# The transposed attention probabilities leave PSUM through two engines, one bank each

## The reference

```
for i in range(6):
    q, k, v = split(shift(x) @ Wqkv[i]);  q, k = rotary(l2norm(q) * qs), rotary(l2norm(k) * ks)
    sim  = q k^T * 8, masked to the 32 keys before each query
    attn = softmax(sim);  x = (attn @ v) @ Wo[i] + x
    x = (a * gelu(gate)) @ W2 + b2 + x,  with a, gate = layernorm(shift(x)) @ W1 + b1
```

## Time and profile before

| what | us |
|---|---|
| median of 3 runs (lowest, highest) | 6509.14 (6506.4, 6510.45) |
| the profiled execution, its own time | 6510.61 |
| its span, first to last instruction | 6508.4 |
| PE busy | 5528.5 (85%) |
| DVE busy | 4359.4 (67%) |
| ACT busy | 3728.3 (57%) |
| POOL busy | 2596.1 (40%) |

### The profile page before, as it was taken

One profiled execution on the slowest core, in us unless ns is written; L12 is line 12 of the kernel. 1 busy time (PEld: TensorE's weight loads), 2 busy tenths in 40 slices (PEclk: granted clock), 3 DMA queues, 4 the chain that ended last, 5 costly groups with the idle time before them and its releaser, 6 DMA issues. The chain is left out here.

```text
span 6508.4 us, 104407 instructions
## 1 busy us (share of the span) xinstructions
PE 5528.5 (85%) x31008; PEld 3051.2 (47%) x31008; DVE 4359.4 (67%) x6942; ACT 3728.3 (57%) x11798; POOL 2596.1 (40%) x2011
## 2 busy tenths in 40 slices
PE   6777777677777999899998999899998999899997
PEld 2333333222224555555555555555555555555553
DVE  6667666433335777777777777777777777777775
ACT  3344434223224676667666666666666666666775
POOL 1111222000003555455555555555555555555553
PEclk9888888777768999999999999999999999999998
DMA  0000000000002222222222222222222222222122
GB/s 37 0 0 0 0 0 0 20 0 0 0 0 81 49 48 49 53 54 48 48 53 50 51 47 49 53 54 47 49 48 56 51 48 48 55 53 48 46 47 65
DMA packets 160227, 244.42 MB, mean 38 GB/s; under 512 B 51280, under 2 KB 51280, under 8 KB 158928
## 3 DMA queue, kind: packets, MB, share of 16 engines
q1 hardware_dynamic: 159696, 238.08, 14.9%
HBM read 30.26 MB, written 6.29 MB: 6 GB/s over the span
## 5 line engine op out<-in xcount | busy, mean ns | idle before, releaser
L323 POOL TENSOR_TENSOR c_Pb<-c_Pb,c_rs 96x512 f32<-96x512 f32 (+1 forms) x960 | 996.9, 1038 | 1406.6 <-DVE c_rs L717 1406.6
L385 ACT ACTIVATE c_Pb<-c_S,c_nb 96x128 f32<-96x128 f32 (+1 forms) x3840 | 1344.0, 358 | 233.1 <-DVE c_nb L708 233.0
L724 DVE COPY c_PTs<-c_S 128x384 f32<-128x384 f32 (+1 forms) x960 | 558.4, 582 | 708.0 <-PE c_S L506 707.0
L396 ACT ACTIVATE c_OT<-c_PO 128x192 f32<-128x192 f32 (+1 forms) x960 | 326.5, 340 | 1072.5 <-PE c_PO L520 1072.0
L335 POOL TENSOR_TENSOR c_rot<-c_tAB 128x1024 f32<-128x1024 f32 x384 | 908.8, 2367 | 0.8 <-DVE c_tAB L687 0.8
L708 DVE TENSOR_REDUCE c_nb<-c_S 96x4 f32<-96x512 f32 (+1 forms) x960 | 656.6, 684 | 239.7 <-PE c_S L496 237.9
L329 POOL TENSOR_TENSOR c_sqs<-c_sq 128x512 f32<-128x512 f32 x384 | 487.6, 1270 | 702.5 <-ACT c_sq L363 702.5
L385 ACT ACTIVATION_READ_ACCUMULATOR c_Pb<-c_S,c_nb 96x1 f32 (+1 forms) x3840 | 756.2, 197 | 0.0
L496 PE MATMUL c_S<-c_QK 64*96 64x128 f32 (+1 forms) x7680 | 667.4, 293 | 0.0
L506 PEld LDWEIGHTS c_S<-c,c_Pb 96*128 96x128 f32 (+1 forms) x3840 | 440.7, 143 | 387.8 <-issue 232.4
L520 PE MATMUL c_PO<-c_PTs,c_V 128*64 128x96 f32 (+1 forms) x7680 | 556.5, 266 | 20.1 <-issue 19.4
(11 more groups left out here) (264 smaller groups left out, 10917.1 us busy)
## 6 DMA issues: line engine op xcount, KB each, us to landing
c_QK<-c_F SPq DMA_DIRECT2D x3072, 64.0 KB, 2.0
c_stage<-in_w_heads SPq DMA_DIRECT2D x36, 256.0 KB, 2.9
c_WT<-in_w_tails SPq DMA_DIRECT2D x6, 537.5 KB, 4.5
b_W<-in_w_level SPq DMA_DIRECT2D x1, 3133.0 KB, 10.3
a_W<-in_w_level SPq DMA_DIRECT2D x1, 3078.0 KB, 10.3
c_WT<-in_w_tails SPq DMA_DIRECT2D x6, 512.0 KB, 3.7
x<-in_x SPq DMA_DIRECT2D x1, 2048.0 KB, 7.4
x_kept<-x SPq DMA_DIRECT2D x1, 2048.0 KB, 6.3
```

The source lines that it names most:

```text
L323: nc.gpsimd.tensor_tensor(p, p, r, ALU.mult).then_inc(*p_ready.up())
L385: e = nc.scalar.activation(Pb[0:m, n % 3, i, :], S[0:m, 2 * (n % 2) + r, c * SPAN_K:(c + 1) * SPAN_K], ACT.Exp, bias=nb[0:m, n % 2, i:i + ...
L724: nc.vector.tensor_copy(PTs[:, n % 2].rearrange("p (b c) q -> p b c q", b=2)[:, :, :, 0:m], S[:, b:b + 2, 2 * SPAN_K:].rearrange("p b (c q ...
```

## The change

`pt_copy` keeps the first bank of the pair (heads `2r + c` with r = 0) on VectorE. The second bank is copied by a new function `pt_move` on ScalarE, with its own semaphore `pt_moved`. `pt_move` stands at the very start of ScalarE's step, ahead of everything that the step had there. TensorE's `scores` and `values` wait for both semaphores.

```
+        pt_moved = sig("pt_moved", NS)
...
+                def pt_move(n, turn):
+                    m, b = query(n % TIMES)[1], 2 * (n % 2)
+                    act.wait_ge(*pt_done.nth(n + 1, turn))
+                    if n >= 2 or not turn.first:
+                        act.wait_ge(*pv_done.nth(n - 1, turn))
+                    nc.scalar.activation(PTs[:, n % 2, 2:4, 0:m], S[:, b + 1, 2 * SPAN_K:].rearrange("p (c q) -> p c q", c=2)[:, :, 0:m], ACT.Copy)\
+                        .then_inc(*pt_moved.up())
...
                     m, tm = back(n, 2, now, prev)
+                    if tm:
+                        pt_move(m, tm)
                     if prev and n == 6:
...
                     if n >= 2 or not turn.first:
                         pe.wait_ge(*pt_copied.nth(n - 1, turn))
+                        pe.wait_ge(*pt_moved.nth(n - 1, turn))
...
                     pe.wait_ge(*pt_copied.nth(n + 1, turn))
+                    pe.wait_ge(*pt_moved.nth(n + 1, turn))
...
-                    nc.vector.tensor_copy(PTs[:, n % 2].rearrange("p (b c) q -> p b c q", b=2)[:, :, :, 0:m],
-                                          S[:, b:b + 2, 2 * SPAN_K:].rearrange("p b (c q) -> p b c q", c=2)[:, :, :, 0:m]).then_inc(*pt_copied.up())
+                    nc.vector.tensor_copy(PTs[:, n % 2, 0:2, 0:m], S[:, b, 2 * SPAN_K:].rearrange("p (c q) -> p c q", c=2)[:, :, 0:m])\
+                        .then_inc(*pt_copied.up())
```

## The result

The changed kernel takes 6875.7 us (6875.5 to 6883.2, 4 runs) against 6509.8 (6506.4 to 6515.5, 4 runs) before: ratio 1.0563, 95% interval 1.0546 to 1.0579. It is 366 us slower; the forecast was 6887, 378 slower. The profiled execution spans 6873.4 us.

What follows compares the result with a forecast made beforehand. The prediction took TensorE to bound the attention part. An ordinary turn's terms summed to 8.45 us; 42 x 8.45 + 5 x 4 + 3.5 = 378 us, from 6510.6 profiled, gave 6887 us, range 6715 to 7070.

Steps and rivals of the forecast that it cites:

- 5 to 10: Steps 5 and 6 together lose 0.15 us a turn, step 7 with its push on step 8 loses 0.95.
- 11 to 14, the stall: Step 11 loses 0.05 us; in steps 12 to 14 copies behind gelus and exponentials cost 3.2 us after absorption.
- 12, the clock: TensorE's idling before step 12's scores lowers its granted clock, costing 1.5 us a turn, bounds 0 and 3.
- What decides: In each of 20 steps, ScalarE's place in its order when transposes end counts, not its 1072 us mean idle time.
- The other steps: Outside steps 11 to 14, terms of 0.4, 1.2, 0.15, 0.95, 0.5 and 0.5 us an ordinary turn.
- VectorE's relief, nothing: VectorE's copy gets 0.2 us shorter 960 times; counted as no gain except where VectorE is late itself, step 8.
- The layer turns, +4 each: The five turns that load a new layer lose 4 us each, between 0 and 8.45.
- The first turn, +3.5: The first turn, which has no feed-forward work, loses 3.5 us.
- A: Rival: no absorption, every delay adds up, 17.9 us in 42 turns, 8 in the others: 7310 us; chance 0.11.
- B: Rival: only the gelus count, delays outside steps 12 to 14 are hidden: 6722 us; chance 0.14.
- D: Rival: nothing changes, gains in seven steps cancel the late ones: 6509 us; chance 0.02.
- C: Rival: faster, ScalarE's idle time takes the copy, both halves end together 0.2 us earlier: 6395 us; chance 0.03.

Runs made afterwards that it cites:

- run 4: The changed kernel with six extra matmuls, their result unread, ahead of the scores of step 12: 6784.3 us, 1.0424 of the kernel before.
- Run 6: The changed kernel with ScalarE's copy directly behind the exponentials of the step before, all 20 jobs still split: 6618.7 us, 1.0170 of the kernel before.
- run 2: The changed kernel, but VectorE copies jobs 10 and 11 (steps 12 and 13) whole: 6680.9 us, 1.0274 of the kernel before.
- Run 10: The kernel before, with VectorE copying only the first bank and no engine the second (zeroed once at the start): 6422.5 us, ratio 0.9864.
- run 1: The changed kernel, but ScalarE copies a bank only in job 10 (step 12), VectorE all else: 6740.0 us, 1.0359 of the kernel before.
- run 8: The changed kernel, but ScalarE copies a bank only in steps 3, 4, 8, 9, 10, 16, 19: 6488.8 us, 0.9966 of the kernel before.

## Why the prediction was right, and where not

The ordinary turn, term by term, beside what the scores of the same steps lose in the changed kernel (means of the 33 turns, against the kernel before, what a later step of the group gives back taken off). Stall and clock are told apart by run 4 (1.98 us in these four steps, 1.93 over the whole turn):

| steps | predicted us | measured us |
|---|---|---|
| 0 and 1 | 0.4 | 0.55 |
| 2 (measured 2 to 4) | 1.2 | 1.05 |
| 5 to 10 | 0.15 + 0.95 | 1.28 |
| 11 to 14, the stall | 0.05 + 3.2 | 2.80 |
| 12, the clock | 1.5 | 1.98 |
| 15 | 0.5 | 0.48 |
| 17 and 18 | 0.5 | 0.46 |
| sum | 8.45 | 8.60 |

- *What decides.* That ScalarE's position at the end of the transposes counts, not its mean load: right. Run 6 has the same copies in another order and takes back 70% of the loss.
- *Steps 11 to 14 and the clock.* The course was right: TensorE idle 5.99 us before the scores of step 12, its wait for `hidden` used up. The stall was put too high by 0.45 and the clock too low by 0.5, and these cancel; that is luck. The clock's price came from a stall of 2.95 us, and the one here is twice as long. From the scores to the next transposes it took 4.72 us in rows 9, and 5.15 on the mean here.
- *The other steps.* Each term came out within 0.2 us, and run 2, with jobs 10 and 11 on VectorE, gives 4.0 for their sum of 3.75.
- *VectorE's relief, nothing.* This step failed. Run 10 gives 1.6 us an ordinary turn, 89 us in all. I had read it from the waits as covered by the projection. Where the scores wait for ScalarE's copy, an earlier end of VectorE's half can't help. But the measured terms of the table contain whatever is left of it, and no run takes it apart in the changed kernel. That the sum came out at 8.60 is therefore partly luck.
- *The layer turns, +4 each.* Wrong: -0.6. Steps 11 and 12 are 3.9 us longer there, near what I said for the whole turn, but others are shorter, step 6 by 1.15, step 14 by 0.7 and step 15 by 1.6. I had reasoned that VectorE is late there, and did not follow that the change relieves VectorE. Run 10 gives 2.1 us for the relief, but it can't be the whole account: job 10 alone costs 5.0 (run 1) and the other copies gain 2.9 (run 2), which adds up to +2.1 and not to -0.6. Single layer turns also scatter, from 102.3 to 105.2 us in run 10. What else shortens them is open.
- *The first turn, +3.5.* Measured 90.6 - 83.3 = 7.3.
- *The total.* The 365 us between the two profiled spans are 359 in the 33 ordinary turns, the eight behind the layer turns and the last one, 7.3 in the first, -3 in the five layer turns, and 1.4 ahead of them all. I had 355, 3.5, 20 and nothing in their places. So the forecast, 12 us too high, owes its miss to the layer turns (23 us too much), and the terms that were too low hid some 10 us of that.
- *The rivals.* A (no absorption, 7310) and B (gelus only, 6722) are out by the time, B also by run 2. D (nothing, 6509) and C (faster, 6395) are out too. But C's mechanism works in a few steps: where ScalarE is free or nearly so, the change gains (run 8). The rule of the Trainium skill that spoke for it, PSUM — Partial Sum Buffer, "Specifications (TRN2)", agrees with the trace of the changed kernel. In 201 of the 768 jobs with 96 queries the two copies overlapped by more than 0.2 us, and took 0.357 us on VectorE and 0.335 on ScalarE. In 302 jobs they didn't overlap at all, and took 0.354 and 0.327.

## What to carry to other kernels

When work goes to a second engine, lay its instruction order beside the moment at which the input is ready, in every step of the loop. The engine's idle time on the mean, 1072 us here, was no guide. In an in-order queue a moved piece can cost twice. It waits for what stands in front of it (here an inverse norm, or gelus with two table loads), and put further ahead it waits for its own input and holds what stands behind. Split the work only in the steps where the second engine is free: here that turned a loss of 5.6% into a gain of 0.3%. And measure what the first engine's relief is worth by itself; a wait that looks covered may still be on the path.

## What the runs showed of the hardware

- A stall of 6.0 us on TensorE in each turn took the granted clock to 0.50 of full (1.2 GHz) and cost 1.93 us a turn beyond the stall itself. Six matmuls whose result nobody reads, put into the stall, kept the clock at 1.00 and made the kernel 91 us faster (6875.7 to 6784.3 us). I hadn't expected filler work to be worth 1.3% of a kernel in which nothing else was changed.
- The price of such a stall isn't fixed. After 6.0 us without a matmul the next stretch of TensorE took 4.90 to 5.86 us in the ordinary turns of the changed kernel, 5.82 on the mean in run 1, and 3.17 with the clock at 1.00.
- An activation table load was 1.283 us, twice in each turn, and the Gelu behind the first one started 0.012 us after its end in all 48 turns.
- One of the extra matmuls of 128x512, whose operands are plain 32-bit floats, shows as two rows and took 0.86 us at a clock of 1.00 (5.31 us for six). A count of the profile's instructions hides this unless one reads "x12" as six matmuls.
